# Windowed attention and a ternary feed-forward on one core: the attention's sums stay with heads on partitions, and their division moves to GpSimd in the feed-forward

## The chip, the core and the metric

The kernel runs on one core of a Trainium2 chip. Its engines are TensorE (PE in the profile, PEld its weight loads), VectorE (DVE), ScalarE (ACT), GpSimd (POOL) and SyncE (SP), which issues nearly all DMAs. The metric is the time of one execution on the device in microseconds, as the median of several.

## The reference

With B=4 sequences of T=2048 tokens, D=256, 16 heads of 16, float32:

```python
x = x + attn(layernorm(x))
x = x + ffn(layernorm(x))
# attn: q, k, v = x @ Wq.T, x @ Wk.T, x @ Wv.T, by head; softmax(q.k / 4) over keys with
#   |i - j| <= 128, and key 0 for every query, and all keys for query 0; weights @ v; @ Wo.T
# ffn:  h = x @ ternary(w_fc).T + gate * (x @ v.T @ fast_b.T @ u.T); relu(h)**2 @ ternary(w_proj).T
```

## The kernel before

Tokens go in 16 groups of 512 (`G`, `GT`). A first stage projects q, k, v and stores them in DRAM. Attention (`stage_attend`) runs over 64 units, each a group and 4 of the 16 heads; `march` writes the stages of successive units into one order on each engine, with the lags `L_MAX` to `L_OUT`. In a unit, TensorE computes 16 small tiles for the row maxima (L1347), which VectorE reads one by one (`dve_tile`, L1362) and gives back; then the scores (L1616), whose exponentials ScalarE writes (L1692), of which GpSimd cuts the corners of the window (L1526), and TensorE forms the weighted sums (L1638) with a column of ones that gives the denominator. Key 0, outside the window for most queries, has its own weight `p0`. VectorE turns the sums in blocks of 32 (L1410), GpSimd adds key 0's part to denominator and numerator (L1538, L1540, L1554), VectorE takes the reciprocal (L1414), GpSimd multiplies (L1572), and the result is stored with tokens on partitions. The shift of a pair of units goes through `rest` (L1535, GpSimd) and ScalarE.

The feed-forward (`stage_feed`) goes through the groups in steps. In one step it works on group `at(0)` (the product with `Wo`: `pe_turn_o` L1844 turns the loaded sums, ScalarE and VectorE split them in a high and a low part, L1921 and L1962, then 24 products, L231 to L233, and the sum with x, L1974), on `at(1)` (the norm: statistics, four small newton steps L167 to L173, scaling L221, turned, L1856), and on `at(2)`: `z` (L1878), and eight slices of the hidden layer, each with products (L1887 to L1892), a relu and its square's high part on ScalarE, the square on GpSimd (L1950), its low part on VectorE (L2004), and the products with the second weight (L1906, L1908). An engine takes its instructions in the written order; semaphores hold it where it needs another's result.

## Time and profile before

| | us |
|---|---|
| median of 3 runs | 1069.56 (1068.85 to 1069.68) |
| profiled execution, its own time | 1071.5 |
| its span, first to last instruction | 1068.9 |
| TensorE busy in the span | 1031.5 (97%) |
| VectorE busy | 921.4 (86%) |
| ScalarE busy | 775.2 (73%) |
| GpSimd busy | 699.6 (65%) |

The granted clock of TensorE is 0.995 of full speed on average. A share over the whole span mixes stages with different limits, so the rows further down are taken from one stage or one step each.

### The profile page before, as it was taken

Reading aid. Unit: us, or ns where it says so; the run is one execution under the profiler, and the core shown is the slowest. Engines: PE = TensorE matmul, PEld = TensorE weight load, DVE = VectorE, ACT = ScalarE, POOL = GpSimd, SP = SyncE. Lnnn points to the kernel's source line nnn. Section 1 sums busy time; section 2 is a strip of 40 time slices with the busy share of each in tenths; the row PEclk is TensorE's granted clock in tenths of the full one; section 3 lists DMA queues with packets and bytes.
Section 4 is the critical chain, followed back from the end, with each engine's and each line's share of the span. In section 5 each row is a group of like instructions: output and inputs, shape, how many; then the busy total and the mean of one; then the engine's idle time right before and its main releaser. Section 6 shows DMA issues by size and latency. Waiting matters only on the chain.

```text
span 1068.9 us, 40083 instructions
## 1 busy us (share of the span) xinstructions
PE 1031.5 (97%) x16071; PEld 789.2 (74%) x16071; DVE 921.4 (86%) x3202; ACT 775.2 (73%) x1328; POOL 699.6 (65%) x945
## 2 busy tenths in 40 slices
PE   9999999799999999999999999999999999999997
PEld 8888887466665666557665666588888888888886
DVE  7889987799999999999999999487888888888885
ACT  7989987687888888887888878854566554556554
POOL 3575556688888888898888888843344443344443
PEclk9999999899999999999999999999999999999999
DMA  6999989878667766776677653512122221123001
GB/s 210 263 314 276 286 231 267 155 136 154 129 139 156 157 126 137 158 145 130 139 138 160 131 120 70 143 38 80 59 89 90 60 60 60 60 79 95 26 21 40
DMA packets 187019, 142.33 MB, mean 133 GB/s; under 512 B 61625, under 2 KB 186577, under 8 KB 186833
## 3 DMA queue, kind: packets, MB, share of 16 engines
q1 hardware_dynamic: 186832, 139.77, 55.3%
q8 instruction: 126, 2.06, 0.9%
q14 instruction: 61, 0.49, 0.2%
HBM read 87.98 MB, written 50.95 MB: 130 GB/s over the span
## 4 chain that ended last, share of the span: by engine, by line
PE 60%; DVE 11%; issue 4%; SPq 3%; ACT 2%; DMA 1%; POOL 0%; DVEq 0%; ACTq 0%
PE e_psum L1616 13%; PE e_psum L1638 12%; PE e_psum L1347 9%; PE e_psum L1906 6%; PE e_psum L1908 6%; DVE a_masked L1362 4%; PE e_psum L1888 3%; PE e_psum L1887 3%; DVE n_stats L144 2%; DVE f_x L2028 2%; SPq L1321 2%; PE e_psum L231 1%; PE e_psum L233 1%; PE e_psum L232 1%; PE e_psum L1892 1%
## 5 line engine op out<-in xcount | busy, mean ns | idle before, releaser
L1692 ACT ACTIVATE a_weights<-e_psum 128x1024 f32<-128x1024 f32 (+1 forms) x512 | 391.4, 809 | 85.2 <-PE e_psum L1616 84.7
L1362 DVE CUSTOM_DVE_ANT_0 a_masked<-e_psum,band 128x290 f32<-128x290 f32 (+1 forms) x992 | 387.7, 445 | 37.9 <-PE e_psum L1347 32.1
L1526 POOL TENSOR_SCALAR_AFFINE_SELECT a_weights<-a_weights 128x1024 f32<-128x1024 f32 x256 | 273.9, 1094 | 48.6 <-ACT a_weights L1692 47.2
L1950 POOL TENSOR_TENSOR f_square<-f_relu 128x512 f32<-128x512 f32 x128 | 147.6, 1154 | 212.8 <-ACT f_relu L1939 189.6
L1347 PE MATMUL e_psum<-e_k,e_q 96*32 96x290 bf16 (+2 forms) x4096 | 236.5, 287 | 15.6 <-DVE max L1362 6.5
L1616 PE MATMUL e_psum<-e_q,e_k 128*32 128x384 bf16 (+2 forms) x5632 | 241.6, 280 | 5.8 <-ACT a_weights L1692 3.6
L1638 PE MATMUL e_psum<-a_weights,a_v 128*17 128x384 f32 (+2 forms) x2816 | 221.7, 389 | 2.0 <-issue 1.4
L1616 PEld LDWEIGHTS e_psum<-e_q,e_k 128*32 128x32 bf16 x5632 | 132.0, 96 | 97.0 <-ACT a_weights L1692 40.9
L1347 PEld LDWEIGHTS e_psum<-e_k,e_q 96*32 96x32 bf16 x4096 | 116.8, 97 | 84.1 <-DVE max L1362 46.7
L1906 PE MATMUL e_psum<-w_w_t,f_square_hi 128*128 128x256 f32 x512 | 129.4, 287 | 4.6 <-DVE f_square_lo L2004 4.6
L1939 ACT ACTIVATE f_relu<-e_psum,w_mag 128x512 f32<-128x512 f32 x128 | 87.4, 683 | 54.5 <-PE e_psum L1892 54.5
L1908 PE MATMUL e_psum<-w_w_t,f_square_lo 128*128 128x256 f32 x512 | 126.7, 282 | 0.0
L2004 DVE TENSOR_TENSOR f_square_lo<-f_square,f_square_hi 128x512 fp32r<-128x512 f32 x128 | 98.7, 790 | 23.7 <-POOL f_square L1950 23.3
L1906 PEld LDWEIGHTS e_psum<-w_w_t,f_square_hi 128*128 128x128 f32 x512 | 96.6, 189 | 14.2 <-DVE f_square_lo L2004 11.2
L1887 PE MATMUL e_psum<-f_xt_hi,w_w_t 128*128 128x512 f32 x256 | 102.7, 401 | 1.1 <-ACT f_relu L1939 1.1
L1888 PE MATMUL e_psum<-f_xt_lo,w_w_t 128*128 128x512 f32 x256 | 101.3, 396 | 0.0
L1908 PEld LDWEIGHTS e_psum<-w_w_t,f_square_lo 128*128 128x128 f32 x512 | 96.8, 189 | 2.8
L1638 PEld LDWEIGHTS e_psum<-a_weights,a_v 128*17 128x17 f32 x2816 | 80.2, 98 | 20.8 <-issue 5.5
L1362 DVE DVE_READ_ACCUMULATOR2_ANT max<- 128x1 f32 x1024 | 84.9, 83 | 0.0
L1942 ACT ACTIVATE f_square_hi<-f_relu 128x512 fp32r<-128x512 f32 x128 | 81.1, 633 | 4.1
L452 POOL TENSOR_TENSOR p_q_parts<-p_rest,p_q_parts 128x512 bf16<-128x512 f32 x32 | 37.8, 1183 | 64.7 <-ACT p_q_parts L655 64.6
L1932 ACT ACTIVATE f_z<-e_psum 128x512 fp32r<-128x512 f32 x16 | 9.6, 597 | 90.6 <-PE e_psum L1879 90.6
(215 smaller groups left out, 1925.3 us busy)
## 6 DMA issues: line engine op xcount, KB each, us to landing
k_parts<-p_k_parts SPq DMA_DIRECT2D x48, 258.0 KB, 4.7
q_parts<-p_q_parts SPq DMA_DIRECT2D x48, 256.0 KB, 5.5
e_q<-q_parts SPq DMA_DIRECT2D x64, 192.0 KB, 4.0
e_k<-k_parts SPq DMA_DIRECT2D x60, 193.5 KB, 3.7
v_ones<-p_va SPq DMA_DIRECT2D x16, 544.0 KB, 5.9
p_x<-in_x SPq DMA_DIRECT2D x16, 512.0 KB, 7.0
e_q<-q_parts SPq DMA_DIRECT2D x64, 128.0 KB, 3.9
f_o<-attention SPq DMA_DIRECT2D x16, 512.0 KB, 4.7
```

Source lines behind the costliest of these rows:

```text
L1347: ins = pe.matmul(self.tile_bank(j)[h * SUB:(h + 1) * SUB, lo:hi], self.qw[u.q][0:SLOT_ROWS, h, j * SUB:(j + 1) * SUB], self.kt[u.hq][0:SL ...
L1362: dve.tensor_tensor_reduce(out=masked[:, place + lo:place + hi], in0=bank[:, lo:hi], in1=self.band[:, lo:hi], scale=1.0, scalar=NEG, op0=A ...
L1526: pool.affine_select(out=blocks, in_=blocks, compare_op=ALU.is_ge, fill=0.0, base=0, pattern=[[0, NQ // 2 * HEAD_COLS // P // CUT_STEP], [ ...
L1616: ins = pe.matmul(score[third // 2][i:i + SUB, c0:c0 + m * P], kt[us.hq][:, h, k0 + i:k0 + i + SUB], qw[us.q][:, h, qb * P:(qb + m) * P], ...
L1638: ins = pe.matmul(sum_bank[32 * j:32 * j + VW, qb * P:(qb + m) * P], vw[:, (up.g * TB + kb) % V_RING, h * VW:h * VW + VW], pe_w[:, up.upar ...
L1692: act.activation(pe_w[:, us.upar, lo:hi], score[c % 2][:], ACT.Exp).then_inc(s_exp, 1)
L1887: pe.matmul(self.h_bank[j % 2][:], lhs, self.sh.xt_hi[:, q.par, k, :], start=(k == 0), stop=False)
L1888: pe.matmul(self.h_bank[j % 2][:], lhs, self.sh.xt_lo[:, q.par, k, :], start=False, stop=False)
L1906: pe.matmul(y, sh.r2_hi[:, j % 4, part], self.w.w2_t[:, j, :], start=(j == 0 and t == 0), stop=False, skip_group_check=True)
L1908: ins = pe.matmul(y, sh.r2_lo[:, j % 4, part], self.w.w2_t[:, j, :], start=False, stop=(j == MH - 1), skip_group_check=True)
L1950: pool.tensor_tensor(sh.r2[:, j % 4, :], sh.r[:, j % 4, :], sh.r[:, j % 4, :], ALU.mult).then_inc(self.s_sq, 1)
L2004: dve.tensor_tensor(sh.r2_lo[:, j % 4, :], sh.r2[:, j % 4, :], sh.r2_hi[:, j % 4, :].bitcast(F32), ALU.subtract).then_inc(self.s_r2lo, 1)
```

## The change

The sums of a unit are no longer turned: VectorE copies them from PSUM to `sums`, heads and columns on partitions, tokens along the row, and they are stored so, denominators too. The weights of key 0 are turned on VectorE, a pair of units at a time, and stored. From both, GpSimd and VectorE form two factors for each head and token (1/denominator, and key 0's weight times it), for three sequences at once at unit 52, for the last one in the feed-forward's steps of groups 5 and 6. DMAs spread each factor over the 16 columns of its head. Three instructions on each half of a group then combine sums, factors and key 0's `v` on GpSimd (`pool_combine`): for groups 0 to 2 in the last nine units of attention, for groups 3 to 15 between the squares of the feed-forward's steps. `pe_turn_o` goes; the split of the attention's result reads SBUF, not PSUM, a step earlier.

```diff
--- before.py
+++ after.py
+        self.sums = sb("sums", [P, 2, GT])
+        self.p0_t = sb("p0_turned", [P, 2, SUB])
+        self.o_t = sb("o", [P, 2, KT, GT])
+        self.factor = sb("factor", [P, 2, KT, GT])
+        self.v0_t = sb("v0", [P, KT, B])
...
+    def load_parts(self, sp, o_dram, p0_dram, batches):
...
+        for n in batches:
+            den, key0 = self.batch_parts(n)
+            rows = o_dram[n * GB:(n + 1) * GB].rearrange("g h e t -> (g h) e t")[:, HD, :]
+            sp.dma_start(den, rows.rearrange("r (s t) -> r s t", t=BATCH_COLS)).then_inc(self.s_parts, DMA)
+            sp.dma_start(key0, p0_dram[n * GB:(n + 1) * GB].rearrange("g h (s t) -> (g h s) t", t=BATCH_COLS)
+                         ).then_inc(self.s_parts, DMA)
+
+    def pool_den(self, pool, last):
+        den, key0 = self.all_parts(last)
+        pool.wait_ge(self.s_parts, DMA * 2 * (B if last else B - 1))
+        pool.tensor_tensor(den, den, key0, ALU.add).then_inc(self.s_factor, 1)
+
+    def dve_factor(self, dve, last):
+        den = self.all_parts(last)[0]
+        dve.wait_ge(self.s_factor, 4 if last else 1)
+        dve.reciprocal(den, den).then_inc(self.s_factor, 1)
+
+    def pool_p0_factor(self, pool, last):
+        rden, key0 = self.all_parts(last)
+        pool.wait_ge(self.s_factor, 5 if last else 2)
+        pool.tensor_tensor(key0, key0, rden, ALU.mult).then_inc(self.s_factor, 1)
+
+    def store_factors(self, sp, factor_dram, batches):
+        sp.wait_ge(self.s_factor, 6 if batches[-1] == B - 1 else 3)
+        for n in batches:
+            for which, part in enumerate(self.batch_parts(n)):
+                sp.dma_start(factor_dram[which, n * GB:(n + 1) * GB].rearrange("g h (s t) -> (g h s) t", t=BATCH_COLS),
+                             part).then_inc(self.s_fout, DMA)
...
-    def dve_sums_turned(self, dve, u):
+    def dve_sums_copied(self, dve, u):
 
         dve.wait_ge(self.s_sum, u.n + 1)
-        wait(dve, self.s_den, u.n - 1)
-        wait(dve, self.s_num, u.n - 1)
-        dve.transpose(self.turned[:, u.upar].rearrange("p b e -> p (b e)"), self.sum_bank).then_inc(self.s_turned, 1)
-
-    def dve_denominators(self, dve, u):
-        dve.wait_ge(self.s_den, u.n + 1)
-        dve.reciprocal(self.rden[:, u.upar], self.den[:, u.upar]).then_inc(self.s_rden, 1)
+        wait(dve, self.s_out[u.upar], u.uhalf * DMA)
+        dve.tensor_copy(self.sums[:, u.upar], self.sum_bank).then_inc(self.s_copied, 1)
+
+    def dve_p0_turned(self, dve, u):
+
+        dve.wait_ge(self.s_p0, u.n + 1)
+        if u.gi == 0:
+            dve.wait_ge(self.s_gate, u.batch * UPG + u.hq + 1)
+        wait(dve, self.s_p0out[u.ppar], u.phalf * DMA)
+        dve.transpose(self.p0_t[:, u.ppar], self.p0[:, u.p0 - 1:u.p0 + 1].rearrange("p a b -> p (a b)")
+                      ).then_inc(self.s_p0t, 1)
...
+                if u := at(L_OUT):
+                    first = 1 if u.gi == 0 else 0
+                    sp.wait_ge(s_copied, u.n + 1)
+                    sp.dma_start(o_dram[u.g].rearrange("(a q) e t -> a q e t", q=UPG)[:, u.hq, :, first:GT],
+                                 sums[:, u.upar, first:GT]).then_inc(s_out[u.upar], DMA)
+                if (u := at(L_SCORE)) and u.n == FACTORS:
+                    sh.load_parts(sp, o_dram, p0_dram, range(B - 1))
+                if (u := at(L_SCORE)) and u.n == FACTORS + 3:
+                    sh.store_factors(sp, factor_dram, range(B - 1))
+                    feed.load_v0(sp, va_dram)
+                    feed.load_o(sp, Group(0))
+                    feed.load_o(sp, Group(1))
+                if (u := at(L_SCORE)) and u.n in (FACTORS + 4, FACTORS + 8):
+                    feed.load_factors(sp, Group((u.n - FACTORS) // 4 - 1))
...
-                if uo:
-                    pool.wait_ge(s_turned, uo.n + 1)
-                    pool.tensor_tensor(den[:, uo.upar], turned[:, uo.upar, :, HD], p0[:, uo.p0], ALU.add
-                                       ).then_inc(s_den, 1)
-                    pool.tensor_tensor(num[:, uo.upar], turned[:, uo.upar, :, 0:HD], t0[:, uo.n % 3], ALU.add
-                                       ).then_inc(s_num, 1)
+                if um and um.n >= 2:
+                    wait(pool, s_p0, um.n - 1)
+                    sh.pool_key0(pool, um, masked)
...
-                    wait(pool, s_num, us.n - 2)
-                    pool.tensor_tensor(
-                        t0[:, us.n % 3], v0[:, us.batch % 2, us.hq * VW:us.hq * VW + HD].unsqueeze(1).broadcast_to([P, SUBS, HD]),
-                        p0[:, us.p0].unsqueeze(2).broadcast_to([P, SUBS, HD]), ALU.mult).then_inc(s_t0, 1)
...
-                if uo:
-                    pool.wait_ge(s_num, uo.n + 1)
-                    pool.wait_ge(s_rden, uo.n + 1)
-                    if uo.hq == 0:
-                        wait(pool, s_out[uo.gpar], stored(uo))
-                    o = ob[:, uo.gpar, :, uo.hq * HD:(uo.hq + 1) * HD]
-                    pool.tensor_tensor(o, num[:, uo.upar], rden[:, uo.upar].unsqueeze(2).broadcast_to([P, SUBS, HD]),
-                                       ALU.mult).then_inc(s_o, 1)
...
+                if us and us.n == FACTORS + 1:
+                    sh.pool_den(pool, False)
+                if us and us.n == FACTORS + 2:
+                    sh.pool_p0_factor(pool, False)
+                if us and us.n >= COMBINED:
+                    g, third = divmod(us.n - COMBINED, 3)
+                    for n in (2 * third, 2 * third + 1):
+                        feed.pool_combine(pool, Group(g), n)
...
-                    for heads in ((0, 1), (2, 3)):
-                        for o in range(len(SUM_ORDER)):
-                            sum_block(o, heads)
+                    for o in range(len(SUM_ORDER)):
+                        sum_block(o, (0, 1))
+                    feed.pe_attention(pe, Group(1), (0,))
+                    for o in range(len(SUM_ORDER)):
+                        sum_block(o, (2, 3))
                     feed.pe_turn_norm(pe, Group(0))
-                    feed.pe_attention(pe, Group(1))
+                    feed.pe_attention(pe, Group(1), (1,))
                     return
...
+                    if us and us.n == UNITS - 3 and j == 12:
+                        feed.pe_attention(pe, Group(0), (0,))
                     if us and us.n == UNITS - 2 and j == 2:
-                        feed.pe_turn_o(pe, Group(0))
-                    if us and us.n == UNITS - 2 and j == 10:
-                        feed.pe_attention(pe, Group(0), (0,))
-                    if us and us.n == UNITS - 1 and j == 2:
                         feed.pe_attention(pe, Group(0), (1,))
-                    if us and us.n == UNITS - 1 and j == TILES - 1:
-                        feed.pe_turn_o(pe, Group(1))
...
                 if um and um.last:
                     dve.wait_ge(s_tile_read, um.n * TILES + TILES)
                     wait(dve, s_rest, um.pair)
                     dve.transpose(mt[:], mx[:, um.ppar, :]).then_inc(s_m, 1)
+                if up and up.last:
+                    sh.dve_p0_turned(dve, up)
                 if uo and uo.n < UNITS - 2:
-                    sh.dve_sums_turned(dve, uo)
-                    if us and us.n == UNITS - 2:
-                        feed.dve_o_high(dve, Group(0))
-                        feed.dve_o_low(dve, Group(0))
-                    if not ux:
-                        sh.dve_denominators(dve, uo)
+                    sh.dve_sums_copied(dve, uo)
+                if us and us.n == FACTORS + 2:
+                    sh.dve_factor(dve, False)
...
+    def load_factors(self, sp, q):
+
+        wait(sp, self.s_comb, q.g * COMBINE)
+        sp.wait_ge(self.sh.s_fout, DMA * 2 * (B if q.batch == B - 1 else B - 1))
+        for k in range(KT):
+            for which in range(2):
+                sp.dma_start(self.sh.factor[:, which, k],
+                             self.factor_dram[which, q.g, k * H // KT:(k + 1) * H // KT].unsqueeze(1)
+                             .broadcast_to([H // KT, HD, GT])).then_inc(self.s_fin_in, DMA)
...
+    def pool_combine(self, pool, q, n):
+
+        k, kind = divmod(n, 3)
+        o, rden, key0 = self.sh.o_t[:, q.par, k], self.sh.factor[:, 0, k], self.sh.factor[:, 1, k]
+        if kind == 0:
+            pool.wait_ge(self.s_oin[q.par], (q.half + 1) * KT * DMA)
+            pool.wait_ge(self.s_fin_in, (q.g + 1) * 2 * KT * DMA)
+            pool.tensor_tensor(o, o, rden, ALU.mult).then_inc(self.s_comb, 1)
+        elif kind == 1:
+            if q.g == 0:
+                pool.wait_ge(self.sh.s_v0, KT * B * DMA)
+            pool.tensor_tensor(key0, key0, self.sh.v0_t[:, k, q.batch:q.batch + 1].broadcast_to([P, GT]), ALU.mult
+                               ).then_inc(self.s_comb, 1)
+        else:
+            pool.wait_ge(self.s_comb, q.g * COMBINE + n)
+            pool.tensor_tensor(o, o, key0, ALU.add).then_inc(self.s_comb, 1)
...
     def _(pool):
-        for g in range(G):
+        def body(at):
+            qn, qf = at(-1), at(LF)
             for j in range(MH):
-                feed.pool_squares(pool, Group(g), j)
+                if qf:
+                    feed.pool_squares(pool, qf, j)
+                if qn and 1 <= j <= COMBINE:
+                    feed.pool_combine(pool, qn, j - 1)
+            if (q := at(0)) and q.g == LAST_PARTS + 1:
+                sh.pool_den(pool, True)
+            if (q := at(0)) and q.g == LAST_PARTS + 2:
+                sh.pool_p0_factor(pool, True)
+
...
             if qa:
-                feed.pe_turn_o(pe, qa, qf)
+                feed.pe_attention(pe, qa, (0,))
...
             if qa:
-                feed.pe_attention(pe, qa)
+                feed.pe_attention(pe, qa, (1,))
...
                 if j == 2 and qa:
-                    feed.dve_o_low(dve, qa)
+                    feed.dve_x1_half(dve, qa, 0)
+                if j == 6 and qn:
+                    feed.dve_o_low(dve, qn, (0,))
                 if j in (3, 4) and qx:
                     feed.dve_scale(dve, qx, range((j - 3) * 2, (j - 3) * 2 + 2))
             if qx:
                 feed.dve_norm_low(dve, qx)
+            if qn:
+                feed.dve_o_low(dve, qn, (1,))
             if qa:
-                feed.dve_x1(dve, qa)
```

GpSimd, the end of attention and the feed-forward, before (`e_` tiles belong to attention, `f_square` is the square):

```order
L1538 TENSOR_TENSOR e_den<-e_turned,e_p 128x16
L1540 TENSOR_TENSOR e_num<-e_turned,e_key_part 128x256
L1572 TENSOR_TENSOR e_o<-e_num,e_rden 128x16x16
L2067 UNCONDITIONAL_BRANCH
L1950 TENSOR_TENSOR f_square<-f_relu 128x512 x128
```

and a piece of a step of the feed-forward in the changed kernel:

```order
L1975 TENSOR_TENSOR f_square<-f_relu 128x512 x3
L1986 TENSOR_TENSOR e_o<-e_o,e_factor 128x512
L1975 TENSOR_TENSOR f_square<-f_relu 128x512
L1990 TENSOR_TENSOR e_factor<-e_factor,e_v 128x512
L1975 TENSOR_TENSOR f_square<-f_relu 128x512
L1994 TENSOR_TENSOR e_o<-e_o,e_factor 128x512
L1975 TENSOR_TENSOR f_square<-f_relu 128x512
L1986 TENSOR_TENSOR e_o<-e_o,e_factor 128x512
```

The 128 squares stood alone; now one of the three combining instructions stands behind each of squares 1 to 6 of a step. The four attention instructions of each unit are gone.

VectorE in a step of the feed-forward, before, from the newton steps on:

```order
L165 RECIPROCAL n_rstd_first<-n_stddev 128x4
L167 TENSOR_TENSOR n_newton<-n_var_eps,n_rstd_first 128x4
L169 TENSOR_TENSOR n_newton<-n_newton,n_rstd_first 128x4
L171 TENSOR_SCALAR n_newton<-n_newton 128x4
L173 TENSOR_TENSOR n_rstd<-n_newton,n_rstd_first 128x4
L2004 TENSOR_TENSOR f_square_lo<-f_square,f_square_hi 128x512
L1962 TENSOR_TENSOR f_o_t_lo<-e_psum,f_o_t_hi 128x512 x2
L2004 TENSOR_TENSOR f_square_lo<-f_square,f_square_hi 128x512
L221 TENSOR_SCALAR f_xn<-f_x,n_meanvar,n_rstd 128x256 x2
```

and after, from the instruction that follows the newton steps:

```order
L2046 TENSOR_TENSOR f_square_lo<-f_square,f_square_hi 128x512
L2016 TENSOR_TENSOR f_x<-e_psum,f_x 128x512
L2046 TENSOR_TENSOR f_square_lo<-f_square,f_square_hi 128x512
L221 TENSOR_SCALAR f_xn<-f_x,n_meanvar,n_rstd 128x256 x2
L2046 TENSOR_TENSOR f_square_lo<-f_square,f_square_hi 128x512
L221 TENSOR_SCALAR f_xn<-f_x,n_meanvar,n_rstd 128x256 x2
L2046 TENSOR_TENSOR f_square_lo<-f_square,f_square_hi 128x512 x2
L2004 TENSOR_TENSOR f_o_t_lo<-e_o,f_o_t_hi 128x512
L2046 TENSOR_TENSOR f_square_lo<-f_square,f_square_hi 128x512
```

The low part of the attention's result had PSUM and SBUF as inputs and stood after the third low part of the squares. It now has two inputs in SBUF, and one half of it stands after the seventh; the sum x1 of the first half (L2016) takes the old place.

TensorE at the same place of a step, before:

```order
L1887 MATMUL e_psum<-f_xt_hi,w_w_t 128x512
L1888 MATMUL e_psum<-f_xt_lo,w_w_t 128x512
L1892 MATMUL e_psum<-f_z,w_u_t 128x512 x2
L1844 MATMUL e_psum<-e_ident,f_o 128x128 x8
L1887 MATMUL e_psum<-f_xt_hi,w_w_t 128x512
```

and after:

```order
L1908 MATMUL e_psum<-f_xt_lo,w_w_t 128x512
L1912 MATMUL e_psum<-f_z,w_u_t 128x512 x2
L231 MATMUL e_psum<-w_wo_hi,f_o_t_hi 128x256
L232 MATMUL e_psum<-w_wo_lo,f_o_t_hi 128x256
L233 MATMUL e_psum<-w_wo_hi,f_o_t_lo 128x256
```

The eight transposes are gone, and twelve of the attention's products (the first three are shown) stand there.

## Rows read from the trace of the kernel before

**Rows 1.** Windows: stretch, us, busy us of each engine (instructions), clock, DMA share, GB/s.

```profile
270.00:701.80 431.80, 415.49 (x10628) 266.65 (x10619) 385.28 (x1822) 348.27 (x550) 374.36 (x563) 1.00 0.66 137
701.80:1024.73 322.93, 318.69 (x2074) 284.35 (x2073) 270.93 (x515) 181.79 (x308) 128.47 (x112) 1.00 0.21 63
```

**Rows 2.** Timeline of TensorE, first products of two steps: start us, us, what.

```profile
817.13 0.39 PE L1878 MATMUL e_psum<-f_xt_hi,w_v_t 128*128 128x512 f32 x1
...
817.60 0.39 PE L1878 MATMUL e_psum<-f_xt_hi,w_v_t 128*128 128x512 f32 x1
...
840.20 0.39 PE L1878 MATMUL e_psum<-f_xt_hi,w_v_t 128*128 128x512 f32 x1
```

**Rows 3.** Timeline of GpSimd in that step; [idle before <-releaser].

```profile
822.37 1.04 POOL L1950 TENSOR_TENSOR f_square<-f_relu 128x512 f32<-128x512 f32 x1 [0.20 <-ACT f_relu L1939]
824.33 1.20 POOL L1950 TENSOR_TENSOR f_square<-f_relu 128x512 f32<-128x512 f32 x1 [0.92 <-ACT f_relu L1939]
826.54 2.29 POOL L1950 TENSOR_TENSOR f_square<-f_relu 128x512 f32<-128x512 f32 x2 [1.01 <-ACT f_relu L1939]
...
833.59 1.37 POOL L1950 TENSOR_TENSOR f_square<-f_relu 128x512 f32<-128x512 f32 x1 [0.88 <-ACT f_relu L1939]
```

**Rows 4.** Timeline of VectorE in that step.

```profile
823.35 1.28 DVE L2004 TENSOR_TENSOR f_square_lo<-f_square,f_square_hi 128x512 fp32r<-128x512 f32 x2
...
824.75 0.80 DVE L167 TENSOR_TENSOR n_newton<-n_var_eps,n_rstd_first 128x4 f32<-128x4 f32 x1
825.58 0.16 DVE L169 TENSOR_TENSOR n_newton<-n_newton,n_rstd_first 128x4 f32<-128x4 f32 x1
...
826.79 1.29 DVE L1962 TENSOR_TENSOR f_o_t_lo<-e_psum,f_o_t_hi 128x512 fp32r<-128x512 f32 x2
827.99 1.39 DVE L2004 TENSOR_TENSOR f_square_lo<-f_square,f_square_hi 128x512 fp32r<-128x512 f32 x1
829.30 1.58 DVE L221 TENSOR_SCALAR f_xn<-f_x,n_meanvar,n_rstd 128x256 f32<-128x256 f32 x2
...
832.78 1.28 DVE L2004 TENSOR_TENSOR f_square_lo<-f_square,f_square_hi 128x512 fp32r<-128x512 f32 x2
```

**Rows 5.** Timeline of TensorE in that step, transposes and products of 256 columns.

```profile
820.39 1.04 PE L1844 MATMUL e_psum<-e_ident,f_o 128*128 128x128 f32 x8
...
826.30 0.28 PE L1906 MATMUL e_psum<-w_w_t,f_square_hi 128*128 128x256 f32 x1
...
826.53 0.28 PE L1906 MATMUL e_psum<-w_w_t,f_square_hi 128*128 128x256 f32 x1
```

**Rows 6.** Timeline of GpSimd and VectorE in the projection stage.

```profile
147.45 1.23 POOL L452 TENSOR_TENSOR p_q_parts<-p_rest,p_q_parts 128x512 bf16<-128x512 f32 x1 [0.66 <-ACT p_q_parts L655]
148.64 1.31 POOL L452 TENSOR_TENSOR p_k_parts<-p_rest,p_k_parts 128x512 bf16<-128x512 f32 x1
...
147.68 1.28 DVE L1095 SCALAR_TENSOR_TENSOR p_masked<-p_masked,z_half,z_below 128x256 f32<-128x256 f32 x1
```

**Rows 7.** Timeline of GpSimd and VectorE at the transition.

```profile
695.03 0.73 POOL L1540 TENSOR_TENSOR e_num<-e_turned,e_key_part 128x256 f32<-128x256 f32 x1
...
695.14 0.64 DVE L173 TENSOR_TENSOR n_rstd<-n_newton,n_rstd_first 128x4 f32<-128x4 f32 x1
```

**Rows 8.** Groups by line, whole span: count | busy us, mean ns | idle before.

```profile
L1410 DVE STREAM_TRANSPOSE e_turned<-e_psum 128x512 f32<-128x512 f32 x64 | 45.0, 704 | 10.8 <-PE e_psum L1638 9.8
...
L1414 DVE RECIPROCAL e_rden<-e_den 128x16 f32<-128x16 f32 x64 | 15.9, 248 | 3.6 <-POOL e_den L1538 3.6
...
L165 DVE RECIPROCAL n_rstd_first<-n_stddev 128x4 f32<-128x4 f32 x16 | 2.7, 166 | 1.0 <-ACT n_stddev L159 1.0
```

**Rows 9.** Timeline of GpSimd in an attention unit.

```profile
407.44 0.25 POOL L1535 TENSOR_TENSOR a_max_rest<-a_max_turned,a_shift 128x32 f32<-128x32 f32 x1
```

**Rows 10.** Timeline of TensorE at the transition.

```profile
697.95 1.16 PE L1856 MATMUL e_psum<-e_ident,f_xn 128*128 128x128 f32 x8 [1.02 <-DVE f_o_t_lo L1962]
```

**Rows 11.** DMA issues in that step: count, KB each, us to landing.

```profile
f_o<-attention SPq DMA_DIRECT2D x1, 512.0 KB, 4.8
```

286 lines of the change are left out of this document (137 added, 149 removed).

## The prediction

> **What bounds the kernel now.** I read the windows of busy time first, since attention and the feed-forward have different limits. From 270 to 701.8 us the kernel is in attention; from 701.8 to 1024.73 it is in the feed-forward, in 14 steps of one group each [rows 1]. There the product `z` of one step starts at 817.13 and that of the next at 840.20: every step takes 23.07 us [rows 2], and 14 of them are the 322.9 us of the window. TensorE is busy for 318.7 of these, so it bounds the step. Counted from start to start, a product of 512 columns takes 0.235 us (two lie between 817.13 and 817.60 [rows 2]), two of 256 columns 0.23 (826.30 to 826.53), so about 0.118 each; eight transposes last 1.04 us, of which I take 0.9, since the end of the last lies under the next product [rows 5]. A step has 44 of the first, 88 of the second and 16 transposes: 10.3 + 10.4 + 1.8 less rounding = 22.4 us, which leaves 0.7 us of waits.
>
> GpSimd is busy for only 128 us of the window [rows 1], so it looks like the place with room. But read the next view, the timeline of GpSimd against VectorE in one step [rows 3, 4]. GpSimd's squares, the second of them at 822.37, run with short gaps to the end of the last at 834.96, and then it idles until the next step. In that stretch VectorE is not free of it: the low part at 827.99 takes 1.39 us where its neighbours take 0.64, and it ends at 829.38, which is 0.55 after GpSimd's pair that began at 826.54 has ended (828.83). The newton step at 824.75, on 4 elements, takes 0.80 us and ends when the square of 824.33 ends (825.53); its twin at 825.58, with GpSimd idle, takes 0.16. The scale pair at 829.30 takes 1.58 for two. The low parts of the attention at 826.79, one input of which is in PSUM, run beside GpSimd at 0.64 each. So a VectorE instruction with two inputs in SBUF, and a `tensor_scalar` in SBUF, wait out a GpSimd instruction that is under way, and the reverse: the square at 833.59 lasts 1.37 instead of 1.04, and ends 0.90 after the second low part of the pair that began at 832.78.
>
> **The change part by part.**
>
> *TensorE in the feed-forward.* Eight transposes leave the step: 21.5 us remain, 1.6 less than the step's 23.07 with its waits. Twelve attention products (1.4 us) now stand between the first low-rank products and the third slice, which hides the wait there. Were this all, 13 steps would give 20 us.
>
> *GpSimd in the feed-forward.* Six instructions of 128x512 are added, one behind each of the squares 1 to 6. The nearest row is the square, 1.04 us when nothing blocks it [rows 3]; I take this, with 0.9 as the lower end (what it shows behind a VectorE end) and 1.3 as the upper (L452 [rows 6], which writes another type). So between square 1 and square 7 twelve instructions stand where six stood, 12.5 us of work in a stretch of 12. GpSimd no longer has gaps there, and each VectorE instruction of the two kinds above finds it at work. That two GpSimd instructions in a row don't shut VectorE out for both is seen in the projection stage: one begins at 147.45, the next is queued at 148.64, and VectorE's L1095 in between ends at 148.96, while the second GpSimd instruction ends at 149.95 [rows 6]. So they take turns.
>
> The timetable of a step, from its `z` at 0. Square 1 ends at 6.3 (822.37 + 1.04 - 817.13). The combination behind it ends at 7.3, and low part 0 0.55 later, 7.9. Square 2, let in after it, ends at 8.8, low part 1 at 9.4. Now come the reciprocal (0.2) and four steps on 4 elements; each ends with the GpSimd instruction under way, and the next of these then begins: 10.3, 11.3, 12.4, 13.4. That such tiny steps are caught one after another is seen at the transition, where the one at 695.14 takes 0.64 us and ends with GpSimd's of 695.03 [rows 7]. Low part 2 ends at 15.0, the sum x1 (PSUM, not blocked) at 15.65, low part 3 at 16.5, the scale pair at 17.9, low part 4 at 18.5, the second pair, each caught, at 20.6, low part 5 at 22.1. Now it ends at 16.3 (the first of the pair at 832.78, 0.64 long, less 817.13). TensorE waits for it, and has behind it 8 + 12 + 8 + 8 products of 256 columns: 4.25 us. The step is then 26.35 us, 3.3 more than 23.07. The 1.6 us of TensorE are no gain any more, since TensorE waits.
>
> Groups 3 to 15 are combined inside steps, 13 of them: +42.6 us. The step after them keeps only TensorE's saving: -1. In one step VectorE also takes the reciprocal of 256 columns. The rows give 166 ns for 4 elements and 248 for 16 [rows 8], so 6.9 ns an element: 1.9 us, of which I take half to lie in a wait for TensorE: +1.
>
> If the newton steps slip through and only low parts and scales are caught, VectorE saves 3.3 us there, but then it meets GpSimd earlier, each of the four scales is caught by itself (1.05) and low part 4 too; laid out in the same way, low part 5 ends at 20.7 and the step is 25.0.
>
> *Attention.* GpSimd loses four instructions of a unit, but nothing in a unit waits for it except the cut weights, which wait for ScalarE: nothing gained. VectorE is busy for 385 of 432 us here [rows 1] and loses the reciprocal, 0.25 us a unit [rows 8]; the transpose of the sums (0.70) becomes a copy of as many columns, which I take as equal; a small transpose comes in every other unit, for which I take 0.2, near the small instructions of these rows. Net -0.15 us over 60 units is -9 at most; TensorE bounds many units itself, and I take -6. Against it stands one reciprocal of 768 columns, put ahead of a unit's tiles: 6.9 ns x 768 = 5.3 us, in which TensorE gets no bank back. Together -1 (from -9 to +5).
>
> *The last nine units* carry the combination of groups 0 to 2 behind the cuts, two a unit, 2.1 us. `rest` (L1535, now at 407.44, right behind the cuts [rows 9]) follows them on GpSimd, and ScalarE waits for `rest` between two exponentials. Three pairs are touched, about 1.3 us each: +4. In return the product of group 0's norm does not wait for L1962 any more (1.02 us [rows 10]) and two sets of transposes (0.9 each) go, partly under ScalarE's work: -2.5. Together +1.5.
>
> *DMA.* The factors of a group are 1 MB in four issues, into one buffer: they start when the last combination of a step has ended (20 in the timetable) and are wanted at 6.3 of the next, 12 us later. A load of 512 KB lands in 4.8 us [rows 11], so twice as much in some 10 at worst. Hidden; if not, each us is lost 13 times. Stores of the sums are awaited two units later: hidden.
>
> Sum: 42.6 - 1 + 1 - 1 + 1.5 = +43. The profiled execution took 1071.5 us with a span of 1068.9; the median of the runs is 1069.6. The difference applies to both; since the timetable takes every catch at its worst moment I take off 3: 1110 on the median's side.
>
> *A page beside the row.* The Trainium skill, GPSIMD Engine Reference, section 3.1, has two-input elementwise work at about 2.6 cycles an element at 1.2 GHz; an estimate from it is 1.11 us for 512 columns where the row shows 1.04. By the page a step would be 0.4 us longer, and the time 5 us.
>
> **The rivals.**
> *The milder catch*: the newton steps pass, 25.0 us a step. For it: three of the four pass now. Against: GpSimd idles at that point now. 13 x 1.95 = 25, and the rest +0.5: 1095.
> *TensorE stays the bound, faster*: VectorE's catches fall where it has slack. It decides when low part 5 ends by 17.2 on the timetable (21.5 - 4.25). Then the step is 21.5 to 21.7, 13 x -1.5 = -20, with the rest 1050. Against it: six low parts stand up to that point, each can be caught for 0.8 us, and only 0.9 us of slack are there.
> *GpSimd keeps its turn*: VectorE gets in only when GpSimd's queue has run dry, so the low parts wait for two instructions. Four catches of 1.04 more a step make it about 30: 1069.6 + 87 = 1157. Against it is the one instance of rows 6. The Trainium skill, SBUF - State Buffer, section Who interferes with whom, says that issue order decides who blocks and that the loser waits for the whole instruction; by that alone this rival would be open, and the trace has the turn-taking only once clearly.
> *No change*: the mild catch with all of the attention gain, within 0.2%: little.
>
> **How the numbers follow.** Forecast 60%, milder 20%, faster 9%, keeps its turn 8%, no change 3%. 0.2% (2 us) is about what a measurement of this kernel tells from no change. Slower has 60 + 20 + 8 = 88%. Range: the forecast's own, with its unknown prices (0.9 to 1.3 a combination is about -12 and +15 in all, attention -8 to +6), is 1098 to 1126; down to the milder case it is 1086 to 1126.
>
> **What would show it.** In the profile after: starts of `z` 25 to 27 us apart; GpSimd without gaps between squares 1 and 7; low parts of 1.4 to 1.6 us, newton steps near 1 us; TensorE waiting for the low part L2046 by 3 to 4 us a step; the new combination at 1.04 to 1.5. In attention one reciprocal of about 5 us. Wrong I would be with steps near 21.6 us (instructions in SBUF not blocked for long), or with waits of GpSimd for the DMA of factors.

## The result

The changed kernel takes 1212.1 us (median of 4 runs, 1206.8 to 1215.3) against 1069.2 for the kernel before in the same session: ratio 1.133, 95% interval [1.129, 1.138]. The forecast was 1110, range 1086 to 1126: slower was right, but about 100 us of the loss were not foreseen. In the changed kernel L1460 is VectorE's copy of a unit's sums, L1552 their store, L1523 the shift rows, L1398 the tiles, L1649 the scores, L1898 `z`, L1975 the squares, L2046 their low parts, and L1986, L1990, L1994 the combination. Windows of the changed kernel, cut where the copy of units 0, 50 and 63 begins, and at the first `z`; columns as in [rows 1]:

```profile
211.40:622.60 411.20, 375.72 (x9775) 238.59 (x9762) 350.99 (x1702) 314.97 (x500) 236.84 (x315) 0.99 0.61 152
622.60:784.00 161.40, 105.93 (x2285) 62.72 (x2286) 87.25 (x342) 76.97 (x118) 82.91 (x90) 0.82 0.37 99
786.56:1211.50 424.94, 367.19 (x2184) 317.35 (x2184) 385.06 (x567) 206.58 (x344) 259.92 (x208) 0.95 0.27 90
```

The same three windows of the kernel before:

```profile
212.40:598.40 386.00, 373.37 (x9786) 239.53 (x9776) 356.67 (x1726) 315.14 (x500) 339.44 (x515) 1.00 0.72 142
598.40:698.50 100.10, 94.70 (x2293) 60.82 (x2285) 79.18 (x348) 77.74 (x120) 82.91 (x120) 1.00 0.54 122
701.80:1068.90 367.10, 356.47 (x2298) 316.62 (x2296) 301.85 (x565) 204.73 (x345) 147.57 (x128) 1.00 0.20 60
```

So of 142.7 us of span, 25.2 come in units 0 to 50, 61.3 in units 50 to 63 and 57.8 in the feed-forward (the rest, -1.6, lies around them). TensorE's busy time rises by only 24 us over all three, partly because its clock falls to the lower level in pieces of the stalls (mean 0.82 in the second window). The rest of the added time TensorE stands still.

**The feed-forward is as forecast.** VectorE and GpSimd of one step, whose `z` begins at 984.84; beside it [rows 3, 4]:

```profile
991.07 1.83 POOL L1986 TENSOR_TENSOR e_o<-e_o,e_factor 128x512 f32<-128x512 f32 x1
992.84 1.50 POOL L1975 TENSOR_TENSOR f_square<-f_relu 128x512 f32<-128x512 f32 x1
994.30 1.04 POOL L1990 TENSOR_TENSOR e_factor<-e_factor,e_v 128x512 f32<-128x512 f32 x1
995.30 1.04 POOL L1975 TENSOR_TENSOR f_square<-f_relu 128x512 f32<-128x512 f32 x1
996.30 1.26 POOL L1994 TENSOR_TENSOR e_o<-e_o,e_factor 128x512 f32<-128x512 f32 x1
...
994.39 0.97 DVE L169 TENSOR_TENSOR n_newton<-n_newton,n_rstd_first 128x4 f32<-128x4 f32 x1
995.39 0.97 DVE L171 TENSOR_SCALAR n_newton<-n_newton 128x4 f32<-128x4 f32 x1
996.39 1.18 DVE L173 TENSOR_TENSOR n_rstd<-n_newton,n_rstd_first 128x4 f32<-128x4 f32 x1
...
1003.35 2.40 DVE L221 TENSOR_SCALAR f_xn<-f_x,n_meanvar,n_rstd 128x256 f32<-128x256 f32 x2
1005.67 2.12 DVE L2046 TENSOR_TENSOR f_square_lo<-f_square,f_square_hi 128x512 fp32r<-128x512 f32 x2
```

Each newton step on 4 elements ends within 0.02 us of the end of one of GpSimd's instructions (994.39 + 0.97 against 994.30 + 1.04), and the next step waits out the next; in steps 2 to 13 all 48 newton steps end within 0.03 us of such an end. TensorE, same step; in brackets its idle time and for whom:

```profile
998.23 0.39 PE L1926 MATMUL e_psum<-w_w_t,f_square_hi 128*128 128x256 f32 x1 [1.96 <-DVE f_square_lo L2046]
...
1007.25 0.38 PE L1926 MATMUL e_psum<-w_w_t,f_square_hi 128*128 128x256 f32 x1 [0.35 <-DVE f_square_lo L2046]
1011.64 0.39 PE L1898 MATMUL e_psum<-f_xt_hi,w_v_t 128*128 128x512 f32 x1
```

On the forecast's timetable: newton steps end at 9.5, 10.5, 11.5, 12.7 (forecast 10.3 to 13.4), low part 4 at 18.6 (18.5), low part 5 about 22.3 (22.1), next `z` at 26.80 (26.35). TensorE waits in four places of the step: 1.96, 0.77 and 0.35 us for low parts, and 1.11 us for the scaled rows (L221).

**Attention is not.** VectorE's and TensorE's waits in units 0 to 47 (us in total, times, longest):

```profile
DVE a_masked L1413 <- PE e_psum L1398: 30.1, 75, 0.9
DVE e_sums L1460 <- DMA attention<-e_sums: 21.5, 16, 4.1
...
PE e_psum L1398 <- DVE max L1413: 27.2, 28, 4.4
```

The copy waits until the store of two units earlier has landed, and as it stands ahead of a unit's tiles, TensorE gets no bank back. Units take 7.7 and 8.8 us in turn (means), where they took 7.6 and 7.9. And in units 51 to 63 (VectorE, TensorE, GpSimd, in order of time):

```profile
626.23 4.95 DVE L1324 RECIPROCAL e_factor<-e_factor 128x768 f32<-128x768 f32 x1 [2.98 <-POOL e_factor L1319]
...
676.13 0.69 DVE L1460 COPY e_sums<-e_psum 128x512 f32<-128x512 f32 x1 [12.36 <-DMA attention<-e_sums]
...
684.42 1.04 PE L1649 MATMUL e_psum<-e_q,e_k 128*32 128x384 bf16 x16 [20.87 <-DMA e_q<-a_shift]
...
683.79 1.26 POOL L1986 TENSOR_TENSOR e_o<-e_o,e_factor 128x512 f32<-128x512 f32 x1 [18.22 <-DMA e_factor<-factors]
...
721.03 1.26 POOL L1986 TENSOR_TENSOR e_o<-e_o,e_factor 128x512 f32<-128x512 f32 x1 [8.13 <-DMA e_factor<-factors]
...
763.58 1.26 POOL L1986 TENSOR_TENSOR e_o<-e_o,e_factor 128x512 f32<-128x512 f32 x1 [11.64 <-DMA e_o<-attention]
```

Ahead of the shift rows that TensorE awaited at 684.42, SP had issued these (start, time to issue, count):

```profile
649.64 4.79 SPq L1335 DMA_DIRECT2D factors<-e_factor  x6
654.48 5.29 SPq L1826 DMA_DIRECT2D e_v<-v_ones  x8
659.80 2.40 SPq L1833 DMA_DIRECT2D e_o<-attention  x4
...
666.83 5.96 SPq L1842 DMA_DIRECT2D e_factor<-factors  x4
672.83 1.82 SPq L1523 DMA_DIRECT2D e_q<-a_shift  x3
```

Issuing late is not all of it: the last of the three rows was issued at 674.06 and landed at 684.38, 10.3 us later, where the median is 2.7. The four loads of factors ahead of it landed one after another up to 683.66.

### The profile page after: what moved, and what is told of

It is laid out like the page before. It is cut to its first block, busy times and chain, and to the rows that moved or that the text cites. A ratio compares the mean times of both kernels' runs of the same rounds, so it can differ in the third digit from the quotient of the medians.

```text
span 1211.6 us, 39704 instructions
## 1 busy us (share of the span) xinstructions
PE 1054.5 (87%) x15943; PEld 789.1 (65%) x15943; DVE 1006.3 (83%) x3174; ACT 776.9 (64%) x1326; POOL 705.9 (58%) x790
## 4 chain that ended last, share of the span: by engine, by line
PE 27%; DVE 21%; DMA 15%; issue 8%; SPq 8%; POOL 3%; ACT 3%; DVEq 0%; POOLq 0%; ACTq 0%
DMA attention<-e_sums 10%; PE e_psum L1649 6%; PE e_psum L1671 6%; DVE f_square_lo L2046 6%; DVE f_xn L221 5%; PE e_psum L1398 5%; SPq L1372 5%; PE e_psum L1926 2%; PE e_psum L1928 2%; DVE a_masked L1413 2%; ACT a_weights L1722 2%; DMA e_factor<-factors 2%; POOL a_weights L1578 1%; DVE n_stats L144 1%; DVE f_x L2070 1%
## 5 line engine op out<-in xcount | busy, mean ns | idle before, releaser
L1722 ACT ACTIVATE a_weights<-e_psum 128x1024 f32<-128x1024 f32 (+1 forms) x512 | 390.9, 808 | 154.7 <-PE e_psum L1649 153.6
L1649 PE MATMUL e_psum<-e_q,e_k 128*32 128x256 bf16 (+2 forms) x5632 | 242.9, 285 | 38.5 <-DMA e_q<-a_shift 23.2
L1398 PE MATMUL e_psum<-e_k,e_q 96*32 96x290 bf16 (+2 forms) x4096 | 235.6, 291 | 43.6 <-DVE max L1413 38.4
L1975 POOL TENSOR_TENSOR f_square<-f_relu 128x512 f32<-128x512 f32 x128 | 156.8, 1225 | 159.6 <-ACT f_relu L1964 159.4
L1649 PEld LDWEIGHTS e_psum<-e_q,e_k 128*32 128x32 bf16 x5632 | 132.9, 98 | 133.1 <-ACT a_weights L1722 51.0
L1398 PEld LDWEIGHTS e_psum<-e_k,e_q 96*32 96x32 bf16 x4096 | 114.2, 98 | 118.2 <-DVE max L1413 81.4
L1926 PE MATMUL e_psum<-w_w_t,f_square_hi 128*128 128x256 f32 x512 | 135.3, 297 | 33.7 <-DVE f_square_lo L2046 33.7
L2046 DVE TENSOR_TENSOR f_square_lo<-f_square,f_square_hi 128x512 fp32r<-128x512 f32 x128 | 128.8, 1025 | 15.8 <-POOL f_square L1975 15.8
L1926 PEld LDWEIGHTS e_psum<-w_w_t,f_square_hi 128*128 128x128 f32 x512 | 100.6, 196 | 50.9 <-DVE f_square_lo L2046 48.4
L1928 PE MATMUL e_psum<-w_w_t,f_square_lo 128*128 128x256 f32 x512 | 131.2, 289 | 0.0
L1908 PE MATMUL e_psum<-f_xt_lo,w_w_t 128*128 128x512 f32 x256 | 105.3, 411 | 0.0
L1928 PEld LDWEIGHTS e_psum<-w_w_t,f_square_lo 128*128 128x128 f32 x512 | 100.8, 197 | 2.5
L1671 PEld LDWEIGHTS e_psum<-a_weights,a_v 128*17 128x17 f32 x2816 | 77.4, 99 | 36.6 <-POOL a_weights L1578 11.0
L1460 DVE COPY e_sums<-e_psum 128x512 f32<-128x512 f32 x64 | 43.1, 673 | 63.1 <-DMA attention<-e_sums 36.2
L1986 POOL TENSOR_TENSOR e_o<-e_o,e_factor 128x512 f32<-128x512 f32 x32 | 52.9, 1652 | 41.5 <-DMA e_factor<-factors 29.8
```

Of the source, the lines that this page charges most:

```text
L1398: ins = pe.matmul(self.tile_bank(j)[h * SUB:(h + 1) * SUB, lo:hi], self.qw[u.q][0:SLOT_ROWS, h, j * SUB:(j + 1) * SUB], self.kt[u.hq][0:SL ...
L1649: ins = pe.matmul(score[third // 2][i:i + SUB, c0:c0 + m * P], kt[us.hq][:, h, k0 + i:k0 + i + SUB], qw[us.q][:, h, qb * P:(qb + m) * P], ...
L1671: ins = pe.matmul(sum_bank[32 * j:32 * j + VW, qb * P:(qb + m) * P], vw[:, (up.g * TB + kb) % V_RING, h * VW:h * VW + VW], pe_w[:, up.upar ...
L1722: act.activation(pe_w[:, us.upar, lo:hi], score[c % 2][:], ACT.Exp).then_inc(s_exp, 1)
L1908: pe.matmul(self.h_bank[j % 2][:], lhs, self.sh.xt_lo[:, q.par, k, :], start=False, stop=False)
L1926: pe.matmul(y, sh.r2_hi[:, j % 4, part], self.w.w2_t[:, j, :], start=(j == 0 and t == 0), stop=False, skip_group_check=True)
```

## The experiments

All start from the changed kernel. The stretches are read from the starts of VectorE's copy of the sums and of `z`; the changed kernel's own runs spread by up to 5 us to either side. It was run in the first session only; the kernel before was run in each, with medians of 1069.2 to 1070.9. The stretches and steps are those of one profiled execution, which can be 6 us from the median (e8). "Later steps" leaves out the step with the reciprocal (27.97 in the changed kernel, 27.84 in e4).

| run | median us | ratio to before, 95% | units 0-50 | 50-63 | first step | later steps |
|---|---|---|---|---|---|---|
| before | 1069.2 | | 386.0 | 100.1 | 23.07 | 23.07 |
| changed | 1212.1 | 1.129-1.138 | 411.2 | 161.4 | 36.31 | 26.80 |
| e1 | 1201.9 | 1.120-1.128 | 405.5 | 157.3 | 36.6 | 26.80 |
| e2 | 1197.6 | 1.116-1.125 | 402.7 | 157.5 | 35.3 | 26.80 |
| e3 | 1202.0 | 1.121-1.128 | 411.1 | 155.0 | 35.2 | 26.80 |
| e4 | 1178.3 | 1.098-1.105 | 409.0 | 154.9 | 34.8 | 22.0-25.6 |
| e5 | 1173.6 | 1.094-1.100 | 385.2 | 149.5 | 32.4 | 26.80 |
| e6 | 1162.2 | 1.083-1.088 | 407.9 | 156.5 | 34.4 | 23.26 |
| e7 | 1212.0 | 1.126-1.134 | 419.4 | 153.2 | 35.9 | 26.80 |
| e8 | 1199.4 | 1.115-1.125 | 408.3 | 146.5 | 35.8 | 26.80 |
| e9 | 1160.2 | 1.079-1.087 | 411.9 | 108.0 | 36.4 | 26.80 |
| e10 | 1178.9 | 1.098-1.104 | 411.5 | 126.8 | 35.7 | 26.80 |
| e11 | 1257.4 | 1.170-1.178 | 448.9 | 164.8 | 40.3 | 26.80 |
| e12 | 1142.7 | 1.064-1.072 | 405.9 | 142.4 | 32.1 | 23.27 |
| e13 | 1197.5 | 1.114-1.122 | 398.6 | 158.0 | 31.9 | 26.80 |
| e14 | 1260.0 | 1.172-1.181 | 450.1 | 173.6 | 36.6 | 26.80 |
| e15 | 1147.3 | 1.067-1.076 | 408.5 | 160.3 | 35.9 | 21.60 |
| e16 | 1191.4 | 1.110-1.118 | 399.7 | 154.7 | 31.4 | 26.80 |
| e17 | 1135.4 | 1.057-1.063 | 400.6 | 145.2 | 27.2 | 23.26 |
| e18 | 1133.6 | 1.055-1.063 | 401.0 | 141.1 | 27.6 | 23.27 |

### The stores of the sums

**e1: four buffers**, two of them in the still unused `o` tile.

```
-        wait(dve, self.s_out[u.upar], u.uhalf * DMA)
+        wait(dve, self.s_out[self.place(u.n)], self.before(u.n) * DMA)   # place: n % 4 up to unit 47
```

> For units 0 to 47 of attention the copies of the sums go through four buffers in place of two; from unit 48 on it is the changed kernel. Theory A (VectorE's copy waits until the store issued two units earlier has landed): its waits for the stores go up to unit 47, the alternation of 7.5 and 8.9 us a unit becomes an even 7.6 to 7.7, and copy 47 comes 18 to 23 us earlier than at 598.9; time 1190 to 1194. Rival B (the stores have twice the bytes and crowd the loads, or VectorE itself has more to do): the periods stay, 1212.

**e2: the store first in SP's turn**, otherwise as the changed kernel.

> Two buffers as in the changed kernel, but SP issues the store of the sums as the first thing of its turn, ahead of the three shift rows and the unit's loads. Theory A1 (the store is late because it stands in SP's queue behind the shift rows and six loads, 2 to 5 us): most of the waits of the copy go, 1192 to 1200. Theory A2 (what is slow is the time from issue to landing, some 6 to 8 us by the packets): the store then shares the DMA engines with fewer loads ahead of it, and about half is gained, 1200 to 1206. Rival B: 1212.

Both take the copy's wait away, and neither brings the time back: 405.5 and 402.7 us for units 0 to 50, where the kernel before takes 386.0. e1 misses its forecast by 8 us; e2's total is inside A1's range, its stretch is not what A1 says. In e1 TensorE waits for loads instead:

```profile
PE e_psum L1682 <- DMA a_v<-v_ones: 12.0, 7, 4.2
PE e_psum L1660 <- DMA e_q<-a_shift: 5.4, 4, 2.5
```

So theory A was half: the store is late, and something also makes SP's loads late.

**e5: half the bytes in the same DMA.**

```
-     [:, u.hq, :, first:GT], sums[:, u.upar, first:GT])
+     [:, u.hq, :, first:GT // 2], sums[:, u.upar, first:GT // 2])
```

> Only the first 256 of the 512 columns of the sums are stored (128 KB a unit instead of 256, in rows of 1 KB); what the feed-forward loads for the other half are other rows, so that its load has the same size. This leaves part of the output out. Two buffers, the order of SP's queue and VectorE's copy are those of the changed kernel. Theory A3 (the bytes of the store, rows that carry nothing included, keep the DMA engines busy: the store lands late, and with four buffers the loads were late instead): the copy's waits of 21.5 us go, TensorE waits for no load, and units 0 to 50 take 7.66 to 7.75 us each as before the change: 20 to 25 us gained, 1187 to 1192. Rival B1 (the place in the queue or VectorE's own work decides, whatever the bytes): at most 5 gained, 1207 to 1212.

Units 0 to 50 are back at 385.2 (before: 386.0), the copy's waits at

```profile
DVE e_sums L1461 <- DMA attention<-e_sums: 1.3, 1, 1.3
```

and the total is down by 38 us, since units 50 to 63 (12) and the first step (4) gain too. That is more than theory A3 gave.

**e11: only the rows that count**, 17 of 32 a head, in four DMAs.

```
+     for j in range(NQ):
+         sp.dma_start(rows[j:j + 1, u.hq, 0:VW, first:GT], sums[j * SUB:j * SUB + VW, u.upar, first:GT])
```

> Each unit's sums are stored by four DMAs of 17 partitions in place of one of 128: 136 KB instead of 256, nothing left out, three more issues for SP (about 0.55 us each). Theory A3 (bytes): as with half the bytes, 20 us and more of units 0 to 50 come back if SP has the time: 1175 to 1190. Rival M (SP is then the bound: 13 issues and its waits do not fit in 7.7 us): the shift rows and loads come late and the time is 1212 or more.

It is 45 us worse, with 136 KB against 256, so bytes as such can't be the cause. (The next expectations call this run the fourth kernel of the third set.) **e13** has ScalarE issue the one store, **e14** the four, **e16** four of 18 rows.

```
-                                 sums[j * SUB:j * SUB + VW, ...
+                                 sums[j * SUB:j * SUB + VW + 1, ...      # e16 against e14: 0:VW + 1 on both sides
```

> The store of the sums, one DMA of 256 KB, is issued by ScalarE at the end of its turn instead of by SP. Theory A4 (the store and SP's loads wait for each other in one queue): the copy's waits and some of TensorE's for SP's loads go; 1190 to 1200. Theory A3 (bytes alone): the same bytes share the same DMA engines, 1205 to 1212. ScalarE's own issue time, some 0.5 us a unit, is a loss where it is the bound: up to 1215.

> As the fourth kernel of the third set (four DMAs of 17 partitions), but issued by ScalarE. Theory M (SP had no time for three more issues, which cost 45 us there): SP now has one issue fewer than in the changed kernel, so most comes back, and with half the bytes 1175 to 1195, if ScalarE can bear four issues, 2 us a unit. Theory N (DMAs of 17 partitions are slow by themselves, or ScalarE becomes the bound): 1220 to 1260 again, and the copy still waits for the stores.

> As the run with four DMAs of 17 partitions issued by ScalarE, with 18 partitions each (36 KB) instead: one row more a head, which nobody reads. Theory P (a DMA of 17 rows runs its rows one after another, as the packets of that run suggest: 68 rows of 84 ns in 5.6 us; 18 rows can be shared out over several DMA engines): the four rows land 3 us or more earlier, the copy's waits go and 50 us or more come back: 1180 to 1200. Rival N (four small DMAs a unit, or ScalarE's issues, are what costs): 1255 to 1265 again.

Moving the store away from SP gives 15 us (e13), but four DMAs of 17 rows stay at 1260 on either engine: SP's time (theory M) is refuted. One row more, and 69 us are gone. In e13, e14 and e16 the stores have a queue of their own, so the trace's packet records can be counted for it (2 KB rows that begin from 300 to 580 us; the last column, over the whole trace, is a count of the 4-byte packets that go with each store):

```
e13 (128 rows):   4590 rows, mean 110 ns; at once 1: 15%, 2: 16%, 3: 21%, 4: 42%, 5: 5% of the time;  4-byte packets a store: 4
e14 (4 x 17):     2108 rows, mean  88 ns; at once 1: 98%, 2: 2%;                                        4-byte packets a store: 1
e16 (4 x 18):     2520 rows, mean 113 ns; at once 1: 24%, 2: 16%, 3: 14%, 4: 12%, 5: 10%, 6 to 9: 25%;   4-byte packets a store: 9
```

The 17 rows run one after another: 68 rows last 5.55 us (473.30 to 478.85), and no unit's do it in less than 5.52. The one store of 128 rows runs with four at once. Its address pattern in DRAM begins with 4 heads, and 17 is prime. The Trainium skill, DMA: Bandwidth & Descriptors, section "Why a DMA increments its semaphore by 16 and not by 1", says how many DMA engines a transfer gets: the largest number up to 16 that divides the slowest dimension of both sides (dimensions of size 1 passed over), so 4, 1 and 9 here. The trace agrees: the 4-byte packets are 4, 1 and 9 a store, and four rows at once is the commonest state in e13. By the same count of rows, from 300 to 580 us of the changed kernel, 44% of the stores' time has four at once, and in steps 2 to 13 of the feed-forward the loads of `o` and of factors, whose pattern begins with 8 heads, have eight at once for 46% of it.

That explains e1, e2 and e5 together: each store keeps four DMA engines busy (e13: 128 rows take 2.8 to 6.5 us from the first to the last, median 4.9), and the parts of SP's loads on these four wait behind it. From issue to landing a store takes 7.5 us (median) in the changed kernel and 4.3 with half the bytes; the 128 KB stores of the kernel before took 3.9.

The landings of a load bear this out. A load of `a_v` tells its semaphore sixteen times that a share of it has landed. Mean time from issue to the 12th, 15th and 16th share (loads issued from 230 to 575 us, 38 to 57 in each trace):

| | stores on | 12th | 15th | 16th |
|---|---|---|---|---|
| before | 16 | 3.1 | 3.4 | 4.0 |
| changed | 4 | 3.5 | 4.3 | 4.7 |
| e5 (half the bytes) | 4 | 3.2 | 3.5 | 4.0 |
| e13 | 4 | 4.7 | 6.0 | 6.3 |
| e14 | 1 | 3.5 | 4.6 | 6.5 |
| e16 | 9 | 3.7 | 4.1 | 4.5 |

In e13 the last four shares come late (the 13th at 5.4), in e14 above all the last one. The trace doesn't name the engine of a share, so that the late ones are those of the store's engines is inferred from their number. A store in another order of dimensions, with 16 engines, was not tried.

In e16 units 0 to 50 still take 13.7 us more than before. No wait for a DMA is left there; TensorE waits for ScalarE, which has four issues in its own order (before, this wait was 0.8 us):

```profile
PE e_psum L1644 <- ACT a_weights L1717: 16.0, 38, 1.7
```

### Units 51 to 63

**e9** leaves out the whole path of the factors in attention, **e10** only what engines compute and wait for.

> Attention without any of the path of the factors: no loads of sums and key 0's part, no addition, reciprocal or product, no stores or loads of factors and no combination of groups 0 to 2 (they are left undivided and without key 0), v0 loaded at units 20 to 23. The feed-forward has all its work and bytes (its factors are loaded from another place for the first three batches). Theory K (the 61 us lost from unit 51 on are this path's, but for the bytes of the stores): units 50 to 63 take 100 to 110 us in place of 161, and the time is 1150 to 1160. Rival L (the end of attention suffers from the doubled store and the loads of o and x): 120 us and more, 1170 to 1180.

> The DMAs of the factors in attention stay, in their places, number and size, but no engine computes with them and GpSimd waits for none: no addition, reciprocal, product or combination of groups 0 to 2 (left out of the result). Theory K1 (SP's 22 issues in a row and the bytes ahead of the shift rows cost most): units 50 to 63 still take 130 to 145 us, 1180 to 1195. Theory K2 (GpSimd's in-order waits for the landing, and the reciprocal, cost most): 105 to 118 us, 1155 to 1168.

By subtraction they split the 61.3 us: 161.4 - 126.8 = 34.6 for the reciprocal and GpSimd's in-order waits, with the combination itself; 126.8 - 108.0 = 18.8 for the 22 DMAs of unit 53 and their like; 7.9 for the stores and the rest. That the parts simply add up is not shown. e10's 126.8 lies between the ranges of K1 and K2, and unit by unit each theory has its place: units 54 and 55 still take 19.5 and 18.5 us (20.1 and 18.6 in the changed kernel), with TensorE waiting 20.9 for the shift rows, while unit 51 falls from 17.1 to 10.6 and units 58, 60 and 62 from 18.1, 12.1 and 19.2 to 7.6, 8.2 and 6.7.

**e8** puts a unit between the issue of the factors of groups 1 and 2 and their first use.

```
+COMBINE_AT = {55: [(0, 0), (0, 1)], 56: [(0, 2), (0, 3)], 57: [(0, 4), (0, 5)],
+              59: [(1, 0), (1, 1), (1, 2)], 60: [(1, 3), (1, 4), (1, 5)], 62: ..., 63: ...}
```

> The combining instructions of groups 1 and 2 stand three a unit at units 59, 60, 62 and 63 in place of two a unit at 58 to 63, so that one unit lies between the issue of a group's factors and their first use. Theory I (GpSimd stands still for the landing of the next factors, which are issued only when the one buffer is free: 8.1 and 11.6 us, and the cuts, rest and scores queue behind): the stalls of units 58 and 60 to 62 (18.1, 12.1, 19.2) lose 15 to 22 us together, 1190 to 1197. Rival J (SP's issues and the shift rows set these stalls, GpSimd's wait is only parallel to them): within 5 us, 1207 to 1212.

14.9 us in the stretch (12.7 on the medians), so theory I holds, at the low end of its size: GpSimd stood still for a transfer issued too late.

**e7** works the factors out batch by batch.

> The factors are worked out batch by batch, at units 19 to 21, 35 to 37 and 51 to 53: three reciprocals of 256 columns and additions of 256 in place of one each of 768, and at unit 53 SP issues two stores of factors in place of six. Theory G (the reciprocal of 768 columns and VectorE's wait for the addition ahead of it, 4.95 + 2.98 us, are lost whole, since TensorE gets no bank back meanwhile): unit 51's 17.1 us falls to 10.5 to 12, two other units rise by 2 to 3.5, and unit 54 loses 2 to 3 of its 20.1 through four issues fewer: 1205 to 1208. Rival H (a queue of DMA issues anywhere costs as much): no gain, 1211 to 1214.

Unit 51 fell to 13.9, the stretch by 8.2, and the two other places gave it back (units 0 to 50 +8.2): rival H. Splitting the stall gained nothing here. **e3** loads v0 and x earlier:

> The eight loads of key 0's v go from SP's turn of unit 53 to the turns of units 20 to 23, two in each; the load of x for group 1 is issued before the last two stores of the sums. Theory C (22 DMA issues, 17.5 us of SP's time, stand ahead of the shift rows that the scores of unit 54 wait for): TensorE's wait of 20.9 us there falls by 5 to 6, and VectorE's wait of 6.7 us for x in the first feed-forward step goes, so that this step takes 29 to 31 in place of 36.3: together 1199 to 1203. Rival D (only the landing of the 3 MB that were issued there counts, the tiny v0 loads cost nothing): only the x part, 1205 to 1207.

6.4 us came in units 50 to 63. The first step gained 1.1, not 6: VectorE's wait for x went, and GpSimd's for the factors of group 3 (9.3 us) was behind it.

### The feed-forward step

**e4** has three combining instructions ahead of the first square and three behind the last; **e6** gives the product with v to ScalarE, and GpSimd's four stand ahead of the first square; **e15** keeps all in place and shortens them to 16 columns (the others stay undivided).

```
+            act.activation(key0, key0, ACT.Copy, scale=self.sh.v0_t[:, k, q.batch:q.batch + 1])   # e6
```

> In each feed-forward step but the first, three of the six combining instructions stand on GpSimd ahead of the first square and three behind the last; factors are loaded in two halves, each when its own buffer is free. Same work, same bytes. Theory E (the prediction's: instructions back to back on GpSimd between the squares hold up the squares and the VectorE instructions with SBUF operands): the step falls from 26.8 to 21.5 to 23 us, TensorE's waits for the low part go, 1150 to 1165. Rival F (the loads of 1 MB of factors a step, or the amount of GpSimd's work whatever its place, slow the step): 26 us and more, 1200 to 1212.

> From group 4 on, the product of key 0's part with v is taken by ScalarE behind the high part of z, and GpSimd's four remaining combining instructions stand ahead of the first square, where GpSimd waits for ScalarE now. Theory E (only GpSimd instructions between the squares, and chains that run through the end of a step, cost time): 21.5 to 21.8 us a step, TensorE's 21.5 the bound, 12 steps by -5.2: 1212 - 62 = 1150, range 1146 to 1158. Rival F1 (the load of 1 MB of factors lands too late for the start of the next step, and GpSimd waits for it): 23 to 25 us a step, 1170 to 1190.

> From group 4 on, each combining instruction works on 16 columns in place of 512, in the same place and with the same waits and DMAs (the rest of the columns stay undivided). Theory E (the time that the combining instructions hold GpSimd and shut VectorE out): 21.5 to 22.0 us a step, 12 steps by -5: 1150 to 1155. Rival O (their number, semaphores, or the loads of factors): 24 to 26.8 us a step, 1180 to 1212.

e15 gives 21.60 us a step: the number, order, semaphores and DMAs of the combination cost nothing, its time on GpSimd costs all 5.2 us (26.80 less 21.60). TensorE's own time, 21.5 in the prediction, is then the bound. e4 missed its forecast by a cost of its own: VectorE's last low part of `o` waited for GpSimd across the step's end, with the next `z` behind it (L1912 <- L2039, 2.2 us a step). In e6 23.26 remain, above the forecast of 21.8 at most. Of the 1.7 us above e15's step TensorE waits 1.2 for low parts (11 steps):

```profile
PE e_psum L1927 <- DVE f_square_lo L2071: 13.6, 11, 1.6
```

### Together

**e12** joins e1, e2, e3, e6 and e8; **e17** has ScalarE's store in place of e2; **e18** also the 18 rows.

> Everything that helped, together: four buffers for the sums up to unit 47, the store first in SP's turn, v0 and x loaded early, a unit between the issue and the use of the factors of groups 1 and 2, and ScalarE's product with GpSimd's four instructions ahead of the first square. If the gains add: 1212 - 50 (feed-forward) - 12 (gap) - 10 (v0, x) - 14 (store) = 1126; since the two changes of the store are for the same wait, and the loads share DMA time, 1125 to 1140. Slower than the kernel before in any case.

> The joined kernel of before, with the store of the sums (one DMA of 256 KB) issued by ScalarE instead of first in SP's turn. If the gain of that move alone (15 us) is another than that of the store first in the turn (14 us) by its share in units 48 on, where the stall of unit 54 and 55 was 8 us shorter: 1130 to 1140. If it is the same: 1140 to 1146.

> The joined kernel with ScalarE's stores, each in four DMAs of 18 partitions (144 KB a unit) in place of one of 128 (256 KB). If bytes are what is left of attention's delay (units 0 to 50 at 400 us against 386 before): 5 to 12 us gained, 1124 to 1131. If what is left comes from ScalarE's issues, as many as 4 a unit, it stays at 1135 or is worse. In either case it is not faster than the kernel before, since units 51 to 63 still carry the factors.

The best, 1133.6 us, is 78 us under the changed kernel and 63 over the one before in its session. e12 is 3 us over its range; e18 against e17 is within the spread. No run here beats the kernel before.

## Why the prediction was right and wrong

- *GpSimd in the feed-forward*: right in mechanism and size, 26.80 against 26.35, so twelve steps give 12 x 3.73 = +44.8, where thirteen were to give 42.6. That the engines take turns is now seen in every one of these steps. TensorE's waits for low parts, 2.6 us a step, are under the 3 to 4 that were to show it, and 0.8 for L221 come on top. The Trainium skill, SBUF — State Buffer, section Who interferes with whom, has issue order decide who blocks, and that fits: each instruction waits out the one under way, and the rival in which GpSimd keeps its turn (30 us a step) did not occur. The step with the reciprocal of 256 columns (1.73 us) took 27.97: +1.2 for +1. The last but one, 21.59, is the -1 (it was -1.5). The steps came out 0.45 us longer than the timetable, so there was nothing to take off for catches at their worst (the sum took off 3).
- *The thirteenth step*, the first, took 36.3 us, which is 9.5 over a later step, and no term of the sum had it. VectorE waited 6.7 us in it for x and GpSimd 3.5 for factors, both behind other DMAs at the end of attention (x took 9.1 us from issue to landing, 785.27 to 794.41).
- *Attention*: VectorE lost the 6 us of busy time as worked out (356.7 to 351.0), and next to nothing of it was time: with the store's cost gone (e5) units 0 to 50 take 385.2 against 386.0. TensorE, busy 373 of 386 us, is the bound, so the -6 was a step that failed, though small. The reciprocal took 4.95 us for 5.3, but VectorE first waited 2.98 for the addition, which was not in the sum.
- *"Stores of the sums are awaited two units later: hidden"* is the first large step that failed: +25 us in units 0 to 50. No price was worked out for the store. The one DMA row at hand, [rows 11], is a load that lands in sixteen shares, and the store's change of shape was not looked at: it begins with 4 heads and runs on four DMA engines, takes 7.5 us to land, and holds up the copy two units on and SP's loads besides. With half the bytes the 25 us are gone (e5).
- *"The last nine units ... Together +1.5"* is the second, with +61 us in units 50 to 63; with it failed the "Hidden" of *DMA* for the loads of factors in attention. In the feed-forward they are hidden, as said: no wait of GpSimd for factors in steps 2 to 13. In attention GpSimd waited three times, with cuts and `rest` queued behind. The first, 18.2 us, was for factors issued behind the other 18 DMAs of the burst. The second, 8.1, was for a load that could be issued only when the one buffer was free, less than a unit ahead of its use. The third, 11.6, ended with the load of `o` that was issued right behind the third group's factors (they landed at 760.24, `o` at 763.50). And the DMAs put ahead of SP's shift rows were not counted: 22 issues, 18.4 us of SP's time, and a landing 7.6 us later than usual. "Wrong I would be with ... waits of GpSimd for the DMA of factors" was the right thing to watch, and it got no rival with a price. The sum had +4 for `rest` and 5.3 for the reciprocal there, and nothing for the DMAs.

## What to carry to other kernels

When a change alters the layout of a DMA, don't price it by bytes: read how many of its rows run at once, and look at the number that its pattern begins with on either side; 17 against 18 rows a DMA was 69 us. List for each new DMA what it is queued ahead of on its issuing engine, and for each single buffer how long lies between "free" and "wanted". Two engines that lock each other out can be forecast instruction by instruction; do the same for the transition, where every engine's order is tight.

## What the hardware showed beyond that

The shape of a small DMA sets much of its time: in e14 34 KB as 17 rows took at least 1.4 us of rows in a line, and four of them held each other up though ScalarE issued them 0.2 to 0.4 us apart. From 300 to 560 us of the changed kernel the median issue took SP 0.43 to 0.58 us, by kind, and the longest 1.9; behind the burst of unit 53 one took 2.5 (four in 5.96 us). TensorE's clock fell in the stalls of attention: behind its 20.9 us of standing still, 16 score products took 1.04 us at 684.42 and 0.60 at 690.13, where the clock was back (the lower level, 1.2 GHz, stands from 665.9 to 689.8). In the feed-forward a fall cost nothing: the steps from 822.87 (mean clock 0.94) and from 984.84 (1.00) both last 26.80 us, since TensorE waits for VectorE in them anyway.
